# Preparation of a cross-attention and FFN kernel: one product of the query and key weights, x in two halves, the first context turned between the groups of x

## The chip, the cores and the metric

The kernel runs on one core of a Trainium2 chip. The time is the device time of one execution in microseconds (us). The core has five engines that run their own instruction streams and meet at semaphores: TensorE (PE; its weight loads are shown as PEld), VectorE (DVE), ScalarE (ACT), GpSimd (POOL) and SyncE (SP), which here only issues the DMAs.

## What is computed

x is 32 batches of 56 tokens of 128 channels; each batch has a context of 1500 rows of 128. The first stage is attention of the normalised x over the context, with a residual:

```python
    def _L0_xattn_ref(x1, x2, x3, Wq, bq, Wk, bk, Wv, bv):
        q = jnp.einsum('bsc,dc->bsd', x1, Wq) + bq
        k = jnp.einsum('bsc,dc->bsd', x2, Wk) + bk
        v = jnp.einsum('bsc,dc->bsd', x3, Wv) + bv
        scores = jnp.einsum('bqd,bkd->bqk', q, k)
        attn = jax.nn.softmax(scores, axis=-1)
        return jnp.einsum('bqk,bkd->bqd', attn, v)
...
    x = x + _L0_xattn_ref(_layernorm(x, axis=-1), ctx_1024, ctx_1024, ...)
    x = x + _L0_ffn_ref(_layernorm(x, axis=-1), ...)
```

The second stage, a gated attention of 16 heads over the 56 tokens, is not touched by the change. The kernel never forms the keys: the scores are (Wk^T(Wq y + bq)) times the context plus a term of bk that is the same along a row. So what the context is multiplied with is "qk", 128 channels by 1792 tokens (32 batches of 56).

## The kernel before

Two batches form a pair; there are 16 pairs. Tokens of batch b of a pair lie on partitions 64b to 64b+55 of `x_all`, pair n in columns 128n to 128n+127. Four pairs are a group (NG = 4 groups). All float32 data that meets the context goes as two float16 parts, high and low, three products each.

Preparation, in the order of the engines' streams:
- GpSimd fills x_all with zeros (L339), makes the identity (L340, L342), fills qT, tmax, p16, aoT and others (L345 to L361). When all groups of x are normalised it multiplies all of them by the key bias (L401), makes the low parts of contexts 0 and 1 (`low_rows`, L366), and after all four low halves of qk copies pair 0's queries (`queries`, L382).
- SP waits for the zeros of x_all, then loads x (L285, 2 x 448 KB), six weights and biases on one semaphore d_w (L289), four contexts (L293 to L295), the weights of the second stage (L309).
- DVE casts the identity (L606, L608), copies bk and, after `d_w`, the bias products (L636); for each group of x statistics and normalisation (`ln_stats`, `ln_apply`, L616 to L631); then the value bias on x (L644), constants diag_h and diag_e (L648, L649), the low half of qk (L652), low parts of contexts 0 and 1 (`split_lo`, L658), evacuation of their transposes (`t_evac`, L664), key bias of all pairs (L748, L750).
- ACT evacuates the two transposed weights (L417, L418), takes the roots (L421), evacuates the transposed x (L424), the queries (L429) and the high half of qk (L433); then casts contexts 0 and 1 (`split_hi`, L439) and evacuates transposes (`t_evac`, L444).
- TensorE transposes Wq and Wv (L923, L924), makes the bias products (L927, L928), transposes the four groups of x (L936), multiplies by Wq (L941), by Wk (L944), waits for all four low halves, and transposes contexts 0 and 1 (`turn`, L965: three chunks of 8 transposes each).

Then `steps(0)`, a loop over i = 1..6 and `steps(7)`, two pairs in each. For a pair: `scores` of its two batches (L980 to L982), the maxima (`tile_max`, L669), their transpose (`max_turn`, L988), the maximum per row and the shifts (`shifts`, m_q L675), `shift` (L996), the exponentials on ACT (`exps`, L450, L452), their low part on GpSimd (`low_probs`, L372), the values of the pair before (L1011 to L1021), and in between the turning of the next pair's contexts (`turn`, `t_evac`, `split_hi`, `split_lo`, `low_rows`). The order in each stream is written out by hand; an engine that waits holds all that stands behind in its stream. A context buffer is loaded again when its three casts are done.

## Time and profile before

| | us |
|---|---|
| time, median of 3 runs (lowest, highest) | 519.33 (518.43, 520.61) |
| the profiled execution | 519.12 |
| its span | 517.2 |
| first score matmul, pair 0 | 43.20 |
| m_q of pair 0 / of pair 3 (L675) | 48.99 / 82.42 |
| last exponentials of the attention start (ACT L452) | 216.00 |

The page gives PE 83% of the span, DVE 85%, ACT 64%, GpSimd 28%, but these are means over stages. In 40 slices of 12.9 us:

```
PE   0456888899888998856879999999999999999975
DVE  4997688888888888557989999999999999999942
POOL 8172477667777677500000000000000000000000
```

Each digit is the busy share in tenths. The first three slices are the preparation, slice 18 the join of the stages. A row of a timeline names the engine, the line, what is written <- what is read, the count of merged instructions, and in brackets how long the engine had been idle and what released it.

### The profile page before, as it was taken

To read this page: it belongs to the slowest core of one execution; us is meant where nothing else is said; L and a number is where in the kernel's file an instruction comes from. 1 tells how busy PE (TensorE), PEld (TensorE's weight loads), DVE (VectorE), ACT (ScalarE), POOL (GpSimd) and SP (SyncE) were. 2 spreads that over 40 slices of the span, in tenths; PEclk is the share of its full clock that TensorE was granted. 3 is DMA by queue.
4 is the path that set the end of the run, shared out by engine and by line. 5 is a ranking of instruction groups with operands and counts; after the bars stand their busy time and mean duration, and the time that the engine had idled before them with its cause. 6 is when DMAs were issued, how large, how long until landed. Compare 5 with 4: busy or idle time off the path is not lost.

```text
span 517.2 us, 25678 instructions
## 1 busy us (share of the span) xinstructions
PE 428.7 (83%) x10768; PEld 365.1 (71%) x10768; DVE 437.6 (85%) x818; ACT 331.6 (64%) x896; POOL 142.9 (28%) x125
## 2 busy tenths in 40 slices
PE   0456888899888998856879999999999999999975
PEld 0225777777777777745768787877878778787864
DVE  4997688888888888557989999999999999999942
ACT  1362776566775667442877678766877668766771
POOL 8172477667777677500000000000000000000000
PEclk9996899999999999977899999999999999999997
DMA  7903345433455430000000000000000000000000
GB/s 164 299 16 111 124 146 179 168 122 122 139 172 167 131 122 3 3 1 1 3 3 6 2 4 4 4 0 4 4 4 4 0 4 4 4 0 4 7 8 10
DMA packets 18125, 29.45 MB, mean 57 GB/s; under 512 B 2988, under 2 KB 13996, under 8 KB 18092
## 3 DMA queue, kind: packets, MB, share of 16 engines
q1 hardware_dynamic: 18092, 28.97, 18.0%
q8 instruction: 25, 0.41, 0.3%
q14 instruction: 8, 0.07, 0.0%
HBM read 28.05 MB, written 0.92 MB: 56 GB/s over the span
## 4 chain that ended last, share of the span: by engine, by line
DVE 49%; PE 31%; issue 13%; ACT 3%; DVEq 1%; DMA 1%; SPq 1%; POOL 1%; ACTq 0%; POOLq 0%
DVE ctxf_all L864 8%; PE ps L965 6%; DVE ctxf_all L838 6%; DVE ah L892 3%; DVE attnf L875 3%; PE ps L996 3%; DVE ctxT L664 3%; PE ps L1171 2%; PE ps L1011 2%; PE ps L1013 2%; PE ps L1012 2%; PE ps L1021 2%; PE ps L980 1%; DVE eq L790 1%; DVE eq L805 1%
## 5 line engine op out<-in xcount | busy, mean ns | idle before, releaser
L366 POOL TENSOR_TENSOR nat<-ctxf_all,nat 128x640 f16<-128x640 f32 x32 | 69.7, 2197 | 50.2 <-ACT nat L439 50.2
L527 ACT ACTIVATE e_sb<-ps,smn 128x56 f32<-128x56 f32 x256 | 76.1, 369 | 1.2 <-DVE smn L882 1.2
L965 PE MATMUL ps<-ident,nat 128*128 128x128 f16 x768 | 61.3, 226 | 11.7 <-DVE ctxT L664 5.5
L439 ACT CAST nat<-ctxf_all 128x1536 f16<-128x1536 f32 x32 | 45.5, 1470 | 39.2 <-PE ps L1013 39.2
L527 ACT ACTIVATION_READ_ACCUMULATOR e_sb<-ps,smn 128x1 f32 x256 | 67.0, 270 | 0.0
L965 PEld LDWEIGHTS ps<-ident,nat 128*128 128x128 f16 x768 | 46.6, 101 | 24.9 <-issue 14.0
L864 DVE TENSOR_TENSOR ctxf_all<-mixp,diag_h 128x3584 f16<-128x3584 f16 x32 | 63.2, 2016 | 0.0
L372 POOL TENSOR_TENSOR p<-pf,p 128x672 f16<-128x672 f32 x32 | 46.1, 1459 | 13.0 <-ACT pf L452 13.0
L444 ACT COPY ctxT<-ps 128x1024 f16<-128x1024 f16 x32 | 33.1, 1034 | 21.8 <-PE ps L965 21.8
L664 DVE COPY ctxT<-ps 128x1024 f16<-128x1024 f16 x64 | 42.6, 684 | 5.0 <-PE ps L965 5.0
L980 PE MATMUL ps<-qk_cur,ctxT 128*128 128x56 f16 x384 | 33.8, 188 | 12.4 <-DVE ctxT L664 10.5
L1106 PE MATMUL ps<-xn,mT 128*128 128x112 f16 x256 | 41.7, 220 | 0.0
L1107 PE MATMUL ps<-xn,mT 128*128 128x112 f16 x256 | 41.6, 220 | 0.0
L1108 PE MATMUL ps<-xn,mT 128*128 128x112 f16 x256 | 41.6, 220 | 0.0
L658 DVE TENSOR_TENSOR nat<-ctxf_all,nat 128x896 f16<-128x896 f32 x32 | 41.2, 1291 | 0.1
L980 PEld LDWEIGHTS ps<-qk_cur,ctxT 128*128 128x128 f16 x384 | 30.7, 96 | 15.1 <-issue 11.7
L1134 PE MATMUL ps<-ctxf_all 128*64 128x224 f16 x768 | 40.0, 260 | 0.7 <-issue 0.6
L1134 PEld LDWEIGHTS ps<-ctxf_all 128*64 128x64 f16 x768 | 36.1, 110 | 2.5 <-issue 1.4
L669 DVE TENSOR_REDUCE tmax<-ps 128x56 f32<-128x672 f32 x32 | 27.1, 850 | 11.2 <-PE ps L982 11.0
L1011 PE MATMUL ps<-p,nat 128*128 128x56 f16 (+1 forms) x384 | 33.4, 187 | 0.9 <-POOL p L372 0.9
L981 PE MATMUL ps<-qk_cur,ctxT 128*128 128x56 f16 x384 | 33.6, 188 | 0.0
L982 PE MATMUL ps<-qk_cur,ctxT 128*128 128x56 f16 x384 | 33.5, 188 | 0.0
...
## 6 DMA issues: line engine op xcount, KB each, us to landing
...
```

The lines of the kernel that those rows point to most:

```text
L366: pool.tensor_tensor(nat[k][:, 1, 7 * C:], ctxf[k][:, 7 * C:], nat[k][:, 0, 7 * C:], ALU.subtract).then_inc(natlo2, 1)
L372: pool.tensor_tensor(p16[:, 1, :, b, 0:S], pf[b][:, :, :], p16[:, 0, :, b, 0:S], ALU.subtract).then_inc(plo, 1)
L439: act.copy(nat[k][:, 0, :], ctxf[k][:, :]).then_inc(nathi, 1)
L527: last = act.activation(e_sb[:, k, b, 0:S], ps[:, b, S * k:S * k + S], ACT.Exp, bias=smn[:, K16 * b + k:K16 * b + k + 1], scale=-1.0, accu ...
L664: dve.tensor_copy(ctxT[b][:, 8 * P * c:8 * P * (c + 1)], ps[:, (3 * b + c) % 2, :].bitcast(F16)).then_inc(tev_d, 1)
L864: last = dve.tensor_tensor(dv[:, part, :, :, :], mixp[:, part, :, :].unsqueeze(2).broadcast_to((P, 2 * NQ, HALF, H)), diag_h[:, :, :].unsq ...
L965: last = pe.transpose(ps[:, (3 * b + c) % 2, :].bitcast(F16)[:, P * (j % 8):P * (j % 8) + P], nat[k][:, j // TK, C * (j % TK):C * (j % TK) ...
L980: pe.matmul(o, hi, qh, start=(t % 6 == 0), stop=False, skip_group_check=True)
L1011: pe.matmul(o, hi, ph, start=(t == 0), stop=False)
L1106: pe.matmul(o, mT[:, 0, h, :], xn16[:, 0, :], start=True, stop=False)
L1107: pe.matmul(o, mT[:, 0, h, :], xn16[:, 1, :], start=False, stop=False)
L1134: last = pe.matmul(o, pj[:, a, k, :], dv[:, b, k, :, 8 * par:8 * par + 8], start=(k % 2 == 0 and a + b == 0), stop=(k % 2 == 1 and a == 1))
```

## The change

The query and key weights are multiplied into one 128 x 128 matrix `wqk` (and Wk^T bq into a column `qk_bias`), so that qk comes from x in one product instead of two; qT and its fill are gone. x is loaded in two halves of eight pairs each, with a semaphore each, behind the weights; DVE fills the second half with zeros, and the fill of x is no longer ahead of the weights' loads. bv has its own load and semaphore, behind context 1. The constants ident16, diag_q, diag_h and diag_e are cast on ACT. Groups 2 and 3 of x are normalised by GpSimd (`apply`). The value bias and the products with the key bias are done by group on GpSimd, those for pair 0 before `steps(0)` and the rest in pairs 0 to 3; the key bias' sum (`key_bias`) is done by group on DVE. The four groups' transposes (`x_turn`) and products (`x_qk`), their evacuations (`x_evac`, `qk_evac`) and low halves (`qk_low`) stand between the pieces of the first contexts' turning; groups 2 and 3 stand in pair 0. GpSimd and DVE have `steps(1)` written out ahead of their loops. The diff, cut (`...` marks what is left out, also within a line):

```diff
@@ semaphores, sync engine @@
-        d_x = sem("d_x")
+        d_x = [sem(f"d_x{h}") for h in range(2)]
+        d_bv = sem("d_bv")
...
+        GC = NP * C // NG
+        T_BANK, Q_BANK = (2, 3, 6, 6), (6, 7, 7, 7)
...
-            sp.wait_ge(c_zero, 1)
-            for b in range(2):
-                sp.dma_start(x_all[SLOT * b:SLOT * b + S, :].rearrange("t (p c) -> t p c", c=C), x_v[b]).then_inc(d_x, 16)
-            for dst, src in ((wq_nat[:, :], wq), (wk_nat[:, :], wk), (wv_nat[:, :], wv),
+            for dst, src in ((wq_nat[:, :], wq), (wk_nat[:, :], wk), (bq_col[:, :], bq.rearrange("(d o) -> d o", o=1)),
...
+            sp.wait_ge(x_zero, 2)
+            for h in range(2):
+                for b in range(2):
+                    sp.dma_start(x_all[SLOT * b:SLOT * b + S, 2 * GC * h:2 * GC * (h + 1)].rearrange("t (p c) -> t p c", c=C),
+                                 x_v[b][:, NP // 2 * h:NP // 2 * (h + 1), :]).then_inc(d_x[h], 16)
...
+            load(0, 0)
+            load(1, 1)
+            sp.dma_start(bv_all[:, :], bv.rearrange("(o d) -> o d", o=1).broadcast_to((P, C))).then_inc(d_bv, 16)
+            load(2, 2)
+            load(3, 3)
@@ gpsimd @@
-            pool.memset(x_all[:, :], 0.0).then_inc(c_zero, 1)
+            pool.memset(x_all[:, 0:2 * GC], 0.0).then_inc(x_zero, 1)
...
-            pool.memset(qT[:, :, :], 0.0).then_inc(c_zero, 1)
...
+                if isinstance(pair, int):
+                    pool.wait_ge(qk_lo, pair // 4 + 1)
                 pool.tensor_copy(qk_cur[s][:, :, :], qk_all[:, :, bass.ds(pair * (2 * S), 2 * S)]).then_inc(qkc, 1)
...
                     low_probs(n + 1, 1, pair)
+                    if isinstance(pair, int) and pair < 4:
+                        add_bv(pair)
+                        if pair < 3:
+                            bias_products(pair + 1)
...
-            pool.tensor_tensor(x2_all[:, :].rearrange("p (n c) -> p n c", c=C), y_all[:, :].rearrange("p (n c) -> p n c", c=C),
-                               bkq[:, 0:C].unsqueeze(1).broadcast_to((P, NP, C)), ALU.mult).then_inc(xbk, 1)
+            def apply(g):
+                pool.wait_ge(ln_rstd, g + 1)
+                for n in range(4 * g, 4 * g + 4):
+                    last = pool.tensor_scalar(y_all[:, C * n:C * n + C], x_all[:, C * n:C * n + C], mv_all[:, 2 * n:2 * n + 1],
+                                              st_rstd[:, n:n + 1], ALU.subtract, ALU.mult)
+                last.then_inc(ln_xp, 1)
+            def bias_products(g):
...
+                pool.tensor_tensor(x2_all[:, k]..., y_all[:, k]..., bkq..., ALU.mult).then_inc(xbk, 1)
+            def add_bv(g):
...
+                pool.tensor_tensor(x_all[:, k]..., x_all[:, k]..., bv_all..., ALU.add).then_inc(c_xbv, 1)
             low_rows(0, 0)
             low_rows(1, 1)
-            pool.wait_ge(su_dve, NG)
             queries(0, 0)
+            apply(2)
+            bias_products(0)
+            apply(3)
             steps(0)
-            with pool.Fori(1, NP // 2 - 1) as i:
+            steps(1)
+            with pool.Fori(2, NP // 2 - 1) as i:
@@ scalar @@
+            act.wait_ge(c_id, 2)
+            act.copy(ident16[:, :], ident[:, :]).then_inc(c_cast, 1)
...
+                act.copy(diag_h[r, :, :], cut.broadcast_to((32, HALF, H))).then_inc(c_cast, 1)
+                act.copy(diag_e[r, :, :], cut.broadcast_to((32, HALF, E // 2))).then_inc(c_cast, 1)
+            act.wait_ge(w_pe, 1)
+            act.copy(wqk[:, :], ps[:, 0, 0:C]).then_inc(w_act, 1)
+            act.copy(qk_bias[:, :], ps[:, 0, C:C + 1]).then_inc(w_act, 1)
+            act.wait_ge(w_pe, 2)
+            act.copy(wvT[:, :], ps[:, 1, 0:C]).then_inc(w_act, 1)
...
+                act.activation(qk_all[:, 0, GW * g:GW * (g + 1)], ps[:, Q_BANK[g], 0:GW], ACT.Identity,
+                               bias=qk_bias[:, 0:1]).then_inc(qk_hi, 1)
...
+            deviations(0)
+            deviations(1)
             split_hi(0, 0, 0)
+            x_evac(0)
+            deviations(2)
+            qk_evac(0)
             split_hi(1, 1, 0)
+            x_evac(1)
+            deviations(3)
             t_evac(0, 0)
+            qk_evac(1)
+            x_evac(2)
             t_evac(1, 1)
+            qk_evac(2)
+            x_evac(3)
+            qk_evac(3)
@@ vector @@
-            dve.tensor_copy(ident16[:, :], ident[:, :]).then_inc(c_dve, 1)
...
+            dve.memset(x_all[:, 2 * GC:], 0.0).then_inc(x_zero, 1)
...
+                dve.wait_ge(d_x[g // 2], 32)
...
-            dve.tensor_tensor(v3(x_all), v3(x_all), bv_all[:, :].unsqueeze(1).broadcast_to((P, NP, C)), ALU.add).then_inc(c_xbv, 1)
...
+                dve.scalar_tensor_tensor(qk_all[:, 1, GW * g:GW * (g + 1)], ps[:, Q_BANK[g], 0:GW], qk_bias[:, 0:1],
+                                         qk_all[:, 0, GW * g:GW * (g + 1)], op0=ALU.add, op1=ALU.subtract).then_inc(qk_lo, 1)
...
                     tile_max(n, pair, 0)
+                    if first:
+                        qk_low(2)
+                        t_evac(1, 1, 2)
                     tile_max(n + 1, pair, 1)
+                    if first:
+                        key_bias(0)
+                        qk_low(3)
...
+                    if isinstance(pair, int) and 0 < pair < 4:
+                        key_bias(pair)
@@ tensor @@
-            pe.transpose(ps[:, 0, 0:P], wq_nat[:, :], ident[:, :])
-            pe.transpose(ps[:, 0, P:2 * P], wv_nat[:, :], ident[:, :]).then_inc(su_pe, 1)
+            pe.matmul(ps[:, 0, 0:C], wq_nat[:, :], wk_nat[:, :], start=True, stop=True)
+            pe.matmul(ps[:, 0, C:C + 1], wk_nat[:, :], bq_col[:, :], start=True, stop=True).then_inc(w_pe, 1)
+            pe.transpose(ps[:, 1, 0:C], wv_nat[:, :], ident[:, :]).then_inc(w_pe, 1)
...
+            def x_turn(g):
+                if g < 2:
+                    pe.wait_ge(ln_x, g + 1)
+                else:
+                    pe.wait_ge(ln_xp, g - 1)
+                    pe.wait_ge(qk_lo, 1)
+                    pe.wait_ge(xt_act, g)
...
+            def x_qk(g):
+                pe.wait_ge(w_act, 1)
+                pe.wait_ge(xt_act, g + 1)
+                if g >= 2:
+                    pe.wait_ge(qk_lo, g)
+                pe.matmul(ps[:, Q_BANK[g], 0:GW], wqk[:, :], xn1T[:, GW * g:GW * (g + 1)], start=True, stop=True).then_inc(qk_pe, 1)
...
                     scores(n + 1, pair, s, 1)
+                    if first:
+                        x_turn(3)
+                        x_qk(3)
+                        pe.wait_ge(qk_lo, NG)
```

TensorE's stream at the start of the program, before (ps is PSUM, ident the identity; L936 x, L941 and L944 the two products, L965 contexts 0 and 1, L980 the first scores):

```order
L923 MATMUL ps<-ident,wq_nat 128x128
L924 MATMUL ps<-ident,wv_nat 128x128
L927 MATMUL ps<-wq_nat,bk_rep 128x128
L928 MATMUL ps<-bq_col,bk_rep 128x1
L936 MATMUL ps<-ident,y_all 128x128 x16
L941 MATMUL ps<-xn1T,wqT 128x448 x4
L944 MATMUL ps<-qT,wk_nat 128x448 x4
L965 MATMUL ps<-ident,nat 128x128 x48
L980 MATMUL ps<-qk_cur,ctxT 128x56
```

The same place in the changed kernel (L1025 x, L1034 the one product, L1052 the contexts, nat0 and nat1 being contexts 0 and 1):

```order
L1012 MATMUL ps<-wq_nat,bk_rep 128x128
L1013 MATMUL ps<-bq_col,bk_rep 128x1
L1025 MATMUL ps<-ident,y_all 128x128 x4
L1052 MATMUL ps<-ident16,nat0 128x128 x8
L1034 MATMUL ps<-xn1T,wqk 128x448
L1052 MATMUL ps<-ident16,nat0 128x128 x8
L1025 MATMUL ps<-ident,y_all 128x128 x4
L1052 MATMUL ps<-ident16,nat0 128x128 x8
L1034 MATMUL ps<-xn1T,wqk 128x448
L1052 MATMUL ps<-ident16,nat1 128x128 x8
```

The groups of x now stand one by one between the chunks of the contexts, and the first scores follow when only groups 0 and 1 and four of six chunks are done.

TensorE between the scores of pair 0's two batches in the changed kernel (L1067 to L1069 are the score matmuls; before, L980 to L982 ran on without anything between):

```order
L1069 MATMUL ps<-qk_cur,ctxT 128x56
L1025 MATMUL ps<-ident,y_all 128x128 x4
L1052 MATMUL ps<-ident,nat 128x128 x8
L1034 MATMUL ps<-xn1T,wqk 128x448
L1052 MATMUL ps<-ident,nat 128x128 x8
L1067 MATMUL ps<-qk_cur,ctxT 128x56
```

Group 2 of x and the last two chunks of context 1 stand there now; group 3 stands behind the second batch's scores.

DVE from the last normalisation to the first maxima, before:

```order
L644 TENSOR_TENSOR x_all<-x_all,bv_all 128x2048
L648 CAST diag_h<-ident 32x448
...
L652 TENSOR_TENSOR qk_all<-ps,qk_all 128x448 x4
L658 TENSOR_TENSOR nat<-ctxf_all,nat 128x896 x2
L664 COPY ctxT<-ps 128x1024 x4
L748 TENSOR_REDUCE cq_x<-x_all 128x16
L750 TENSOR_SCALAR cq<-cq_x,bkq 128x16
L669 TENSOR_REDUCE tmax<-ps 128x56 x2
L675 TENSOR_REDUCE m_q<-ps 128x1
```

DVE in the changed kernel from the statistics of group 3 to m_q (L688 to L695 statistics, L729 `t_evac`, L723 `split_lo`, L711 `qk_low`, L734 `tile_max`, L716 and L718 `key_bias`, L740 m_q):

```order
L695 TENSOR_SCALAR st_ve<-mv_all 128x4
L729 COPY ctxT<-ps 128x1024
L723 TENSOR_TENSOR nat<-ctxf_all,nat 128x896
L700 RECIPROCAL st_rstd<-st_std 128x4
L711 SCALAR_TENSOR_TENSOR qk_all<-ps,qk_bias,qk_all 128x448
L729 COPY ctxT<-ps 128x1024
L734 TENSOR_REDUCE tmax<-ps 128x56
L711 SCALAR_TENSOR_TENSOR qk_all<-ps,qk_bias,qk_all 128x448
L729 COPY ctxT<-ps 128x1024
L734 TENSOR_REDUCE tmax<-ps 128x56
L716 TENSOR_REDUCE cq_x<-x_all 128x4
L718 TENSOR_SCALAR cq<-cq_x,bkq 128x4
```

The value bias and the constants are gone from DVE, one batch's maxima stand between the low halves of groups 1 and 2, and the key bias' sum is a quarter as wide.

## Rows read from the trace of the kernel before

**Rows 1.** Busy time by stage: start:end, length, per engine busy (instructions), clock, DMA, GB/s.
```profile
0.00:43.00 43.00, 17.23 (x85) 11.53 (x86) 32.42 (x79) 14.56 (x24) 22.78 (x32) 0.93 0.63 175
...
60.00:290.00 230.00, 195.53 (x4638) 168.31 (x4635) 189.76 (x373) 147.50 (x268) 114.14 (x88) 0.96 0.26 84
```

**Rows 2.** Chain of waits, first 60 us: start, us, what.
```profile
6.98 4.93 DMA bv_all<-in_L_xattn_bv_dram
...
13.76 0.79 DVE bst_all L616 x4
...
16.66 1.11 DVE y_all L631 x4
...
24.29 2.29 DVE x_all L644
26.58 4.62 DVE diag_h L648
...
33.00 2.22 DVE qk_all L652 x4
35.22 3.70 DVE nat L658 x2
...
44.14 2.20 DVE cq_x L748
...
48.99 0.30 DVE m_q L675
```

**Rows 3.** Timeline: start, us, engine, line, what, count, idle before and releaser.
```profile
3.17 1.80 POOL L345 MEMSET qT<- 128x2048 f32 x1
3.25 5.02 DVE L606 CAST ident<-ident 128x128 f16<-128x128 f32 x1 [3.25 <-POOL ident L342]
...
24.41 6.54 POOL L401 TENSOR_TENSOR x_all<-y_all,bkq 128x2048 f32<-128x2048 f32 x1 [12.01 <-DVE y_all L631]
...
31.36 0.38 DVE L648 CAST diag_h<-ident 32x448 f16<-32x448 f32 x1
```

**Rows 4.** Timeline, the loads of x on SP's queue.
```profile
2.57 0.96 SPq L285 DMA_DIRECT2D x_all<-in_x_dram  x2
```

**Rows 5.** DMA issues: KB each, median us from issue to landing.
```profile
fws_nat<-in_L_ffn_Ws_dram SPq DMA_DIRECT2D x1, 64.0 KB, 2.8
```

**Rows 6.** Busy time by stretch, columns as in rows 1.
```profile
4.00:10.00 6.00, 0.00 (x0) 0.00 (x0) 4.49 (x3) 0.00 (x0) 5.83 (x18) 1.00 1.02 175
10.00:22.00 12.00, 3.54 (x14) 2.66 (x14) 8.49 (x50) 2.50 (x8) 2.40 (x4) 1.00 1.05 339
...
38.00:44.00 6.00, 4.32 (x49) 4.04 (x50) 3.45 (x5) 1.84 (x3) 1.14 (x1) 0.50 0.75 255
...
48.00:54.00 6.00, 5.14 (x32) 3.71 (x33) 4.06 (x8) 1.60 (x2) 0.16 (x1) 0.50 0.26 77
...
60.00:62.00 2.00, 1.98 (x72) 1.86 (x69) 1.41 (x6) 1.57 (x2) 0.03 (x1) 1.00 0.04 8
```

**Rows 7.** Timeline of TensorE's weight loads, and its transposes at 39.66 us.
```profile
26.71 0.34 PEld L941 LDWEIGHTS ps<-xn1T,wqT 128*128 128x128 f32 x1 [0.41 <-issue]
...
28.05 0.19 PEld L941 LDWEIGHTS ps<-xn1T,wqT 128*128 128x128 f32 x1 [0.18 <-issue]
...
39.66 3.75 PE L965 MATMUL ps<-ident,nat 128*128 128x128 f16 x32 [2.27 <-DVE ctxT L664]
```

**Rows 8.** Instructions on tile ctxf_all up to 45 us: duration ns min/median/max.
```profile
L366 POOL TENSOR_TENSOR nat<-ctxf_all,nat x2: 1402/1818/2234, 34.4 to 35.7; 128x640 f16<-128x640 f32 x2
```

**Rows 9.** Timeline of ACT, 40 to 56 us.
```profile
43.50 2.85 ACT L439 CAST nat<-ctxf_all 128x1536 f16<-128x1536 f32 x2
52.38 1.01 ACT L444 COPY ctxT<-ps 128x1024 f16<-128x1024 f16 x1 [6.04 <-PE ps L965]
```

**Rows 10.** Timeline of DVE and of GpSimd in pairs 2 and 3.
```profile
70.31 0.86 DVE L669 TENSOR_REDUCE tmax<-ps 128x56 f32<-128x672 f32 x1 [0.71 <-PE ps L982]
...
72.80 2.32 POOL L366 TENSOR_TENSOR nat<-ctxf_all,nat 128x640 f16<-128x640 f32 x1 [2.92 <-ACT nat L439]
```

More of the change, by code:

```diff
@@ L699, in result @@
                 after(dve, x2c, pair)
+                if isinstance(pair, int) and pair < 4:
+                    dve.wait_ge(c_xbv, pair // 4 + 1)
                 after(dve, prj, pair + 1)
@@ L902, in iteration @@
                     second(i + 1)
-            dve.wait_ge(c_zero, 22)
+            dve.wait_ge(c_zero, 21)
+            dve.wait_ge(c_cast, 11)
             dve.wait_ge(x2c, NP)
@@ L1057, in steps @@
                         turn(n + 3, 1, k1, (2,))
-            for b in range(2):
-                turn(b, b, b)
+            x_turn(0)
+            pe.wait_ge(c_cast, 1)
+            pe.wait_ge(w_act, 3)
+            pe.wait_ge(bkq_out, 1)
+            turn(0, 0, 0, (0,))
+            x_qk(0)
+            turn(0, 0, 0, (1,))
+            x_turn(1)
+            turn(0, 0, 0, (2,))
+            x_qk(1)
+            turn(1, 1, 1, (0,))
+            pe.wait_ge(c_zero, 9)
             steps(0)
```

180 lines of the change are left out of this document (93 added, 87 removed).

## The prediction

> **What bounds the kernel now.** I read the busy shares by stage first, then the chain of waits, then the timelines of the engines on it. The kernel has a preparation of 43 us, sixteen pairs of attention up to about 215 us, and a second stage. In the preparation no engine is full: DVE is busy 32 of 43 us, PE 17, ACT 15 [rows 1]. From 60 us on DVE and PE hold each other above 80%, and the change leaves the code of that stretch alone but for four pairs. So the time to win is the time before the first pair.
>
> The chain [rows 2] says why the preparation is long: it goes through DVE nearly all the way. After the landing of the last weight (11.9 us) DVE normalises x, then does on the path, among other things, the value bias on all of x (2.29), the casts of the constants (4.62 for the first alone), the low half of the queries for all pairs (2.22), both low halves of the contexts (3.70), and the key bias of all pairs (2.20); for three of these five pair 0 needs only a quarter of it, or nothing yet. The reduction of pair 0's maxima, m_q, starts at 48.99. I take it as the end of the preparation and ask when it starts afterwards.
>
> The 4.62 and a 5.02 us cast at 3.25 us are stalls, not work: the same cast takes 0.38 when GpSimd is idle, and both long ones lie under GpSimd's own instructions, a row of fills and a 6.54 us multiply [rows 3].
>
> **The loads.** Before, SP waits for the fill of x_all and issues x at 2.57 us, the weights after it, 0.48 us each [rows 4]. Now five weight loads go first and wait for nothing. I start them at 0.75 us, where the first fill starts today: issued by 3.1. A small weight load takes 2.8 us from issue to landing [rows 5], so the last one is there at about 5.4 instead of 11.9. Packets of x move at 175 GB/s, those of the contexts at 339 and more [rows 6]. x in two halves of 0.46 MB behind the weights, stream starting at 4.2, 2.6 us each, 0.8 us for the landing (an estimate: from the last packets to the release at 11.9): halves at 7.6 and 10.2, context 0 (0.77 MB, 2.1 us at an estimated 370, since the 339 holds smaller packets too) at 12.2, context 1 at 14.3. The bias load bv now stands behind context 1; its reader is GpSimd in pair 0, much later.
> Fresh here is the fill of x's second half on DVE. No row shows a DVE fill. Lower bound: half of GpSimd's 1.80 for 2048 columns [rows 3], 0.9 us, done before SP gets there at 3.1, so free. Upper bound: it is held like the cast, until GpSimd's row of fills pauses (8.27 us before; 5.6 now, since 1.8 us of qT and 0.9 us of x are gone), which makes x 2.5 us later. I take free, as a fill reads nothing; the held case is a rival. The Trainium skill, "VectorE: DVE Perf Modes", section "Zero memsets can be issued as uint32 (trn2)", has such a fill at one cycle per element, by which it would be an estimated 1.1 us; no run here shows it.
>
> **Weights and x.** The two transposes become one product of the weights, the product with bq and one transpose; two evacuations become three small ones. They fall in 5.4 to 7.6 us where all wait for x: nothing. Then DVE's first two statistics and first normalisation, 4.1 us (13.7 to 17.8 [rows 2]): y of group 0 at 11.7, 6.1 us earlier than now. ACT's casts of constants (about 4 us) run from 2.4 us on, and w_pe is waited for only after: hidden by the loads; without that cover they would cost those 4 us.
>
> **The interleaved part.** Here each engine waits for the next, in order, so I followed the instruction order of the new kernel with today's durations. At the low clock, as PE has it at 26 us (weight loads of the 448-column product 0.74 apart, 0.37 at the high clock, each the load and the idle time ahead of it; two loads per product [rows 7]), x_qk takes 1.5, at the high clock 0.75. Eight context transposes take 0.94 (32 in 3.75 [rows 7], at 0.50 of the clock) or an estimated 0.6, 36 score matmuls 1.0 at the high clock (72 in 1.98 [rows 6]) or an estimated 1.7.
> ACT casts context 0 at 12.2 to 13.7 (two take 2.85 [rows 9]). Then x_qk(0) ends 16.3, its evacuation and low half 17.8 (0.6 each, as the four low halves in 2.22 [rows 2], and a release of 0.1 to 0.2 ahead of each). DVE normalises group 1 till 16.7, so x_turn(1) ends 18.6. DVE's statistics of group 3 end at 19.9, and ACT's deviations(3) waits for them with t_evac(0,0) behind it: till 21.1. x_qk(1) ends 21.0, its low half 22.5, t_evac(1,1,0) 23.2. scores(0) can start at about 22.
> Between scores(0) and scores(1) now stands new work: x_turn(2), a context turn, x_qk(2), their evacuations, low half and t_evac, and behind scores(1) the same for group 3, with max_turn waiting for all four low halves. At the low clock throughout: scores(1) 29.7 to 31.4, x_turn(3) to 32.7, x_qk(3) to 34.9, low half 36.3, m_q at 36.9. With the clock up from 21 us (PE is busy nearly without gap from 14 on): scores(1) ends 28.8, low half 32.7, m_q 33.3. I take 35.0 between them, as there are gaps of over 1 us while DVE and ACT work. **Gain: 48.99 - 35.0 = 14.0 us**, bounds 12.1 and 15.7.
>
> **What is late next.** The casts of contexts 2 and 3 stood at 43.5 us [rows 9], well ahead of m_q. Now they stand behind qk_evac(3), so the low half of context 2 meets GpSimd's part of it. In such a meeting the GpSimd part took up to 2.23 us, the lone one 1.40 [rows 8], and DVE's two 3.70 [rows 2]: 0.2 to 1.4 us, I take 0.8. t_evac of context 2 on ACT was already 3.4 us behind m_q [rows 9], so the rest keeps its distance.
> Here the Trainium skill speaks against the change ("SBUF — State Buffer", section "SBUF: two separate sides"): GpSimd and a DVE instruction with two SBUF inputs or in its fast mode take one port pair in turn, the later blocked for the whole instruction. The trace agrees: one context pair serialised. By that rule nothing in my sum is free where the added GpSimd pieces meet split_lo, and the sum would be nearer its upper bounds.
>
> **In pairs 0 to 3.** key_bias(1..3) puts a reduction of 512 columns and a small add, some 0.9 us by the 2.20 for 2048, ahead of tile_max. The second tile_max waits 0.71 us for PE [rows 10], which covers most: 0.2 each, 0.6 together; bounds 0 and 2.7. The seven quarter pieces on GpSimd (add_bv, bias_products): 512 columns cost 1.12 by the lone 1.40 for 640, 1.64 by the 6.54 for 2048. Two per pair are 2.2 to 3.3, and GpSimd waits 2.92 per pair [rows 10]: 0 to 0.4 for each of three, I take 0.5 in all. apply(2) and apply(3) end well ahead of x_turn(2) and (3).
> PE ran at 1.2 GHz through 48 to 54 us [rows 6]; if it comes in warm this saves up to 2 us of transposes and shifts; I take 0.5.
>
> **Sum.** 519.1 us of the profiled execution (span 517.2; the median is 519.3, so the same): -14.0 + 0.8 + 0.6 + 0.5 - 0.5 = -12.6, **506.5 us**.
>
> **Rivals.**
> The fill is held: x at 10.1, everything behind it 2.5 later: 509.0. For: the 5.02 us cast. Against: it reads nothing. Chance 0.12.
> The interlock binds: clock low to the end and every meeting at its dearer bound: -12.1 + 1.4 + 1.4 + 1.1 + 0: 510.9. For: the clock at 38 to 44 us was 0.50 [rows 6]; many hops, each of which can lose 0.1 us of release. Chance 0.22.
> The clock rises early and stays: -15.7 + 0.2 + 0.3 + 0 - 1.5: 502.4. For: PE denser than today. Against: the waits for groups 2 and 3. Chance 0.13.
> It doesn't do what it says: the first pairs wait for something else (contexts 2 and 3, the ones in order behind them) and the gain is given back, within 0.5%: 519. Against: all four contexts landed by 19 us by the rates above. Chance 0.03.
> Slower: GpSimd becomes the bound in pairs 0 to 3. Its pieces delay low_rows of the next contexts, and PE's third turn waits for these. Today it has 2.9 us to spare; to eat the 14 us over four pairs its two pieces would need 2.9 + 3.5 = 6.4 us, 3.2 each; for 0.5% slower, 3.9 each: 522. The dearest row gives 1.64. Chance 0.02.
> The forecast keeps 0.48.
>
> **Numbers.** Range 502 to 511.5: it reaches from the early clock to the interlock, and allows for the join of the two stages (214 to 256 us), where a shift by 13 us meets the clock's changes elsewhere. 0.5% is 2.6 us, about what a measurement can tell: faster 0.95, same 0.03, slower 0.02.
>
> **What would show it.** x's first statistics on DVE at about 7.6 us (10.1: held fill). No long cast on DVE. First scores at 21 to 23 us. scores(1) 6 to 8 us behind scores(0). m_q at 33 to 37. The same distance of m_q from pair to pair as before from pair 4 on, and pairs 1 to 3 within 0.5 of it; if they take more, look whether GpSimd's wait ahead of low_rows is gone. The forecast is wrong if the context casts on ACT start well behind 12.2 us, or if PE waits for qk_lo longer than 4 us ahead of max_turn.

## The result

The changed kernel takes 510.15 us (median of 4 runs, 509.59 to 512.48) beside 519.97 for the kernel before in the same comparison: ratio 0.983, 95% interval 0.981 to 0.986. Its profiled execution took 509.82 us, with a span of 508.0. So 9.3 us are gone between the two profiled executions, where 12.6 were predicted; 510 lies inside the range of 502 to 511.5, at its slow end.

The stages, against [rows 1] (start:end, length, per engine busy (instructions), clock, DMA, GB/s):

```profile
0.00:43.00 43.00, 22.69 (x194) 16.74 (x194) 27.34 (x74) 21.91 (x37) 23.92 (x42) 0.88 0.67 195
60.00:290.00 230.00, 194.45 (x4735) 166.76 (x4733) 194.12 (x373) 148.37 (x296) 110.85 (x87) 0.97 0.23 77
```

DVE does 5 us less and ACT 7 us more in the first 43 us, and TensorE is turning pair 1's contexts by then. The chain of waits of the changed kernel (start, us, what), where [rows 2] had DVE:

```profile
4.55 0.46 SPq L299
5.05 0.88 SPq L304
5.97 0.32 SPq L305
6.34 6.55 DMA ctxf_all<-in_ctx_dram
12.91 1.48 ACT nat L501
...
15.54 1.61 PE ps L1034 x2
17.24 0.64 ACT qk_all L494
17.91 0.68 DVE qk_all L711
...
24.71 0.99 PE ps L1025 x4
...
34.58 0.30 DVE m_q L740
34.90 1.40 DVE nshift L742
36.33 1.37 DVE dg L746
```

Up to 12.9 us it is now the loading of context 0; of x only the issuing of its loads is on it (L299), not its landing. Then it passes between ACT, PE and DVE, and m_q of pair 0 stands at 34.58: 14.4 us ahead of before, where 14.0 was predicted. The rest of the story is behind m_q. Its two followers, nshift and dg, which take 0.22 and 0.25 us in a quiet pair, took 1.39 and 1.36.

Start of m_q (us) in the two kernels, and its distance to the next:

| pair | before | after | lead | distance before | distance after |
|---|---|---|---|---|---|
| 0 | 48.99 | 34.58 | 14.41 | 11.73 | 14.04 |
| 1 | 60.72 | 48.62 | 12.10 | 10.87 | 11.58 |
| 2 | 71.59 | 60.20 | 11.39 | 10.83 | 10.83 |
| 3 | 82.42 | 71.03 | 11.39 | 10.83 | 11.89 |
| 4 | 93.25 | 82.92 | 10.33 | 10.84 | 11.61 |
| 5 | 104.09 | 94.53 | 9.56 | 10.86 | 10.83 |
| 15 | 212.06 | 202.45 | 9.61 | | |

So 4.8 us are given back in pairs 0 to 4, 2.3 in pair 0 and 2.5 in the next four, and nothing later; from the last m_q to the end of the span it is 305.1 us before and 305.5 after.

### The profile page after: what moved, and what is told of

It is laid out like the page before. It is cut to its first block, busy times and chain, and to the rows that moved or that the text cites. A ratio compares the mean times of both kernels' runs of the same rounds, so it can differ in the third digit from the quotient of the medians.

```text
span 508.0 us, 25659 instructions
## 1 busy us (share of the span) xinstructions
PE 424.5 (84%) x10763; PEld 362.0 (71%) x10763; DVE 428.5 (84%) x805; ACT 333.6 (66%) x904; POOL 149.6 (29%) x139
## 4 chain that ended last, share of the span: by engine, by line
DVE 48%; PE 30%; issue 14%; ACT 4%; DVEq 1%; DMA 1%; SPq 1%; POOL 0%; ACTq 0%; POOLq 0%
DVE ctxf_all L947 8%; DVE ctxf_all L921 6%; PE ps L1052 6%; DVE ah L975 3%; DVE attnf L958 3%; DVE ctxT L729 3%; PE ps L1083 3%; PE ps L1279 2%; PE ps L1098 2%; PE ps L1099 2%; PE ps L1100 2%; PE ps L1108 1%; DVE oh L894 1%; DVE eq L873 1%; DVE eq L888 1%
## 5 line engine op out<-in xcount | busy, mean ns | idle before, releaser
L379 POOL TENSOR_TENSOR nat<-ctxf_all,nat 128x640 f16<-128x640 f32 x32 | 67.0, 2110 | 45.4 <-ACT nat L501 45.2
L1052 PE MATMUL ps<-ident,nat 128*128 128x128 f16 x768 | 61.0, 225 | 11.7 <-DVE ctxT L729 3.4
L1052 PEld LDWEIGHTS ps<-ident,nat 128*128 128x128 f16 x768 | 46.4, 100 | 27.1 <-issue 16.1
L1067 PE MATMUL ps<-qk_cur,ctxT 128*128 128x56 f16 x384 | 34.3, 189 | 12.8 <-DVE ctxT L729 10.8
L729 DVE COPY ctxT<-ps 128x1024 f16<-128x1024 f16 x64 | 42.8, 685 | 2.4 <-PE ps L1052 2.4
L723 DVE TENSOR_TENSOR nat<-ctxf_all,nat 128x896 f16<-128x896 f32 x32 | 42.1, 1315 | 1.3 <-ACT nat L501 1.2
L1067 PEld LDWEIGHTS ps<-qk_cur,ctxT 128*128 128x128 f16 x384 | 30.9, 96 | 15.6 <-issue 10.5
L1214 PE MATMUL ps<-xn,mT 128*128 128x112 f16 x256 | 40.3, 217 | 0.0
L1215 PE MATMUL ps<-xn,mT 128*128 128x112 f16 x256 | 40.1, 216 | 0.0
L1216 PE MATMUL ps<-xn,mT 128*128 128x112 f16 x256 | 40.1, 216 | 0.0
L734 DVE TENSOR_REDUCE tmax<-ps 128x56 f32<-128x672 f32 x32 | 27.0, 851 | 11.0 <-PE ps L1069 11.0
L1068 PE MATMUL ps<-qk_cur,ctxT 128*128 128x56 f16 x384 | 34.0, 188 | 0.0
L1069 PE MATMUL ps<-qk_cur,ctxT 128*128 128x56 f16 x384 | 34.0, 188 | 0.0
```

The lines of the kernel that those rows point to most:

```text
L379: pool.tensor_tensor(nat[k][:, 1, 7 * C:], ctxf[k][:, 7 * C:], nat[k][:, 0, 7 * C:], ALU.subtract).then_inc(natlo2, 1)
L723: dve.tensor_tensor(nat[k][:, 1, 0:7 * C], ctxf[k][:, 0:7 * C], nat[k][:, 0, 0:7 * C], ALU.subtract).then_inc(natlo, 1)
L729: dve.tensor_copy(ctxT[b][:, 8 * P * c:8 * P * (c + 1)], ps[:, (3 * b + c) % 2, :].bitcast(F16)).then_inc(tev_d, 1)
L1052: last = pe.transpose(ps[:, (3 * b + c) % 2, :].bitcast(F16)[:, P * (j % 8):P * (j % 8) + P], nat[k][:, j // TK, C * (j % TK):C * (j % TK) ...
L1067: pe.matmul(o, hi, qh, start=(t % 6 == 0), stop=False, skip_group_check=True)
L1214: pe.matmul(o, mT[:, 0, h, :], xn16[:, 0, :], start=True, stop=False)
```

## Where the 4.8 us go: two engines at one time

The timelines of DVE and of GpSimd behind m_q of pair 0 in the changed kernel (start, us, engine, line, what, count, idle before and releaser):

```profile
34.58 0.29 DVE L740 TENSOR_REDUCE m_q<-ps 128x1 f32<-128x128 f32 x1 [0.42 <-PE ps L1075]
34.90 1.39 DVE L742 SCALAR_TENSOR_TENSOR nshift<-m_q,cq 128x1 f32<-128x1 f32 x1
36.33 1.36 DVE L746 TENSOR_SCALAR dg<-diag_q,nshift 128x56 bf16<-128x56 f32 x1
37.73 0.30 DVE L748 SCALAR_TENSOR_TENSOR dg<-diag_q,nshift,dg 128x56 bf16<-128x56 f32 x1
...
34.88 2.76 POOL L379 TENSOR_TENSOR nat<-ctxf_all,nat 128x640 f16<-128x640 f32 x2 [5.91 <-ACT nat L501]
```

GpSimd had sat idle for 5.91 us, waiting for ACT's casts of contexts 2 and 3, and began its two low parts (1.38 each) 0.02 us ahead of nshift. nshift ends when the first of them ends, dg when the second does. Each works on one or 56 columns; the 2.3 us are the wait for GpSimd.

In pair 3 it is the order of two starts that decides. First pair 3 of the changed kernel, then pair 4, then pair 5, from when on the distances are the old ones:

```profile
71.36 0.39 DVE L742 SCALAR_TENSOR_TENSOR nshift<-m_q,cq 128x1 f32<-128x1 f32 x1
...
72.26 2.29 DVE L723 TENSOR_TENSOR nat<-ctxf_all,nat 128x896 f16<-128x896 f32 x1
...
72.18 3.64 POOL L379 TENSOR_TENSOR nat<-ctxf_all,nat 128x640 f16<-128x640 f32 x2 [0.45 <-ACT nat L501]
...
83.90 1.48 DVE L748 SCALAR_TENSOR_TENSOR dg<-diag_q,nshift,dg 128x56 bf16<-128x56 f32 x1
...
83.91 3.74 POOL L379 TENSOR_TENSOR nat<-ctxf_all,nat 128x640 f16<-128x640 f32 x2 [1.68 <-ACT nat L501]
...
106.52 1.09 DVE L723 TENSOR_TENSOR nat<-ctxf_all,nat 128x896 f16<-128x896 f32 x1
...
106.56 4.52 POOL L379 TENSOR_TENSOR nat<-ctxf_all,nat 128x640 f16<-128x640 f32 x2 [2.92 <-ACT nat L501]
```

In pair 5 DVE comes 0.04 us ahead, takes 1.09, and GpSimd waits at no cost (the same in the kernel before: DVE's low half at 72.77 with 1.08, and GpSimd at 72.80 [rows 10]). In pair 3 GpSimd comes 0.08 us ahead and DVE's low half takes 2.29. Pair 1 is the same (GpSimd 0.04 us ahead, the low half 2.30), and pair 2, with the same added work, escapes by 0.05 us. In pair 4 the two meet one instruction earlier: the second part of dg takes 1.48 where it takes 0.28 in pair 5. Its start is 0.01 us ahead of GpSimd's in the profile, which is too little to say who was first. The shift is small: ACT's cast, which releases GpSimd, began 0.35 us ahead of m_q in such a pair before, and 0.41 ahead in pair 3 now. DVE in turn is late by `key_bias` or by a GpSimd piece (nshift took 0.39). GpSimd's idle time ahead of these low parts, 2.92 us in both kernels' quiet pairs, is 0.45 in pair 3.

By the Trainium skill ("SBUF — State Buffer", section "SBUF: two separate sides") an instruction of GpSimd and one of DVE that wants the shared port pair lock each other out for a whole instruction, and whoever starts first has it. The trace agrees: 1.39 us for nshift beside a GpSimd instruction of 1.38 that had begun 0.02 us earlier, and 1.09 or 2.29 for the same low half by who came first. Pair 4, above, neither bears this out nor speaks against it.

My theory from here, **A**: the missing 3 us are these meetings, so they come back when GpSimd's low parts, or its pieces, stand elsewhere. The rival, **B**: pairs 0 to 4 are late by something else on their way (the late casts and turnings of contexts 2 and 3, or the added `key_bias` sums on DVE), and a held instruction only fills a wait.

## Experiments on the first pairs

Each kernel is the changed one with the edit shown, unless it says otherwise. The changed kernel itself was run a second time, in one comparison with "contexts 2 and 3 cast earlier", "GpSimd told to wait" and "the pieces of pairs 0 to 3": 508.71 us, ratio 0.982 (0.979 to 0.985), m_q of pair 0 at 34.33 and the distances as above within 0.01 us. The experiments of this section differ from it by about 2 us, and only for the pieces is the interval of the ratio apart from its own. So the readings below rest on the distances between the m_q, from one profile for each kernel, and not on the times.

**Contexts 2 and 3 cast earlier.** ACT casts them between the evacuations of qk (and no longer in pair 0; that part of the edit isn't shown), so that GpSimd's low parts fall ahead of m_q.

```diff
             qk_evac(1)
+            split_hi(2, 2, 0)
             x_evac(2)
             t_evac(1, 1)
             qk_evac(2)
+            split_hi(3, 3, 0)
             x_evac(3)
```

> ACT casts contexts 2 and 3 in its idle times of pair 0 (behind qk_evac(1) and qk_evac(2)), not behind qk_evac(3). Theory A, the port: in pair 0 DVE's two small instructions nshift (1.39 us, else 0.22) and dg (1.36, else 0.25) are held by GpSimd's low parts of contexts 2 and 3, which start 0.3 us behind m_q; with the casts early GpSimd is done before m_q, both take their usual time, m_q of pair 1 comes 2.3 us earlier (46.3), and the time falls by 2.0 to 2.5 us (ratio 0.979). Rival B, the clock and the table: pair 0 is long because TensorE runs at half clock and ACT loads a table; then m_q of pair 1 moves by less than 0.5 us.

Measured: 506.93 us, ratio 0.976 (0.972 to 0.981); m_q 34.26, 45.89, 57.47. Behind m_q of pair 0:

```profile
34.59 0.22 DVE L745 SCALAR_TENSOR_TENSOR nshift<-m_q,cq 128x1 f32<-128x1 f32 x1
34.84 0.25 DVE L749 TENSOR_SCALAR dg<-diag_q,nshift 128x56 bf16<-128x56 f32 x1
...
28.99 2.77 POOL L379 TENSOR_TENSOR nat<-ctxf_all,nat 128x640 f16<-128x640 f32 x2
```

Pair 0's distance fell from 14.04 to 11.63 (11.73 before the change), the others stayed at 11.58, 10.82, 11.88, 11.62. All 2.4 us of pair 0 go with the meeting. The time fell by 1.8 us, where 2.0 to 2.5 were expected.

**GpSimd told to wait.** That kernel also moves the casts. Here the casts stay, and GpSimd alone starts its low parts in pair 0 later, behind dg.

```diff
+                        if first:
+                            pool.wait_ge(dgr, 1)
                         low_rows(n + 2, (2 * s + 2) % 4)
```

> In pair 0 GpSimd waits for the end of DVE's shifts before the low part of context 2. Theory A, the port: nshift and dg take 0.22 and 0.25 us, the low part of GpSimd comes 1 us later and now meets DVE's low part, so 1.0 to 2.3 us are won in pair 0 and m_q of pair 1 comes at 46.3 to 47.6. Rival B: the two are slow for another reason (their operands, the first use): they stay at 1.4 us each, and the time stays or rises.

Measured: 506.84 us, ratio 0.978 (0.974 to 0.981); pair 0's distance 11.57.

```profile
34.31 0.22 DVE L744 SCALAR_TENSOR_TENSOR nshift<-m_q,cq 128x1 f32<-128x1 f32 x1
34.56 0.25 DVE L748 TENSOR_SCALAR dg<-diag_q,nshift 128x56 bf16<-128x56 f32 x1
34.85 0.28 DVE L750 SCALAR_TENSOR_TENSOR dg<-diag_q,nshift,dg 128x56 bf16<-128x56 f32 x1
35.04 1.08 DVE L725 TENSOR_TENSOR nat<-ctxf_all,nat 128x896 f16<-128x896 f32 x1
...
35.21 4.38 POOL L379 TENSOR_TENSOR nat<-ctxf_all,nat 128x640 f16<-128x640 f32 x2 [6.47 <-DVE dg L750]
```

Nothing was moved ahead, an engine was made to wait, and pair 0 lost 2.5 us all the same (1.0 to 2.3 were expected). GpSimd's two low parts now take 4.38 instead of 2.76, at no cost in pair 0. This separates A from B for pair 0: it was neither the late casts nor the turning. But pair 2 of this kernel took 11.74 us instead of 10.83: there GpSimd came 0.08 us ahead of DVE's low half, which took 2.29, the meeting that pair 2 of the changed kernel had escaped. From pair 0 to pair 5 the gain is 1.5 us, and not 2.5.

**The pieces of pairs 0 to 3.** GpSimd does the key bias products of groups 1 to 3 and the value bias of group 0 ahead of `steps(0)`, and the other value biases one pair earlier.

```diff
             apply(3)
+            bias_products(1)
+            bias_products(2)
+            bias_products(3)
+            add_bv(0)
             steps(0)
...
-                    if isinstance(pair, int) and pair < 4:
-                        add_bv(pair)
-                        if pair < 3:
-                            bias_products(pair + 1)
+                    if isinstance(pair, int) and pair < 3:
+                        add_bv(pair + 1)
```

> The four products with the key bias and the first value-bias piece are done by GpSimd in its idle 6 us before pair 0's low parts; pairs 0 to 2 keep one value-bias piece each, the key-bias sums on DVE stay. From m_q of pair 1 to that of pair 5 the changed kernel takes 45.9 us where the kernel before takes 43.4. Theory A, GpSimd's pieces: they hold a small DVE instruction or push DVE's low part behind GpSimd's; without most of them at least half of the 2.5 us is gone, and the time falls by 1.3 to 2.5. Rival B, the key-bias sums on DVE (0.9 us in each of three pairs): they stay, so the 45.9 stays within 0.4.

Measured: 506.69 us, ratio 0.977 (0.974 to 0.979); from m_q of pair 1 to that of pair 5 44.35 us, where it was 45.91 after the change and 43.37 before. So 1.6 of the 2.5 us went with these pieces. Pair 4 still took 11.61. But a piece that is moved meets DVE where it lands, here ahead of m_q:

```profile
31.86 2.19 DVE L720 TENSOR_SCALAR cq<-cq_x,bkq 128x4 f32<-128x4 f32 x1
33.96 0.67 DVE L713 SCALAR_TENSOR_TENSOR qk_all<-ps,qk_bias,qk_all 128x448 f16<-128x448 f32 x1
...
29.06 3.73 POOL L432 TENSOR_TENSOR x_all<-y_all,bkq 128x512 f32<-128x512 f32 x3
32.74 1.28 POOL L443 TENSOR_TENSOR x_all<-x_all,bv_all 128x512 f32<-128x512 f32 x1
```

A 4-column instruction (0.23 in the changed kernel) was held for the rest of one GpSimd piece and the whole of the next, and m_q of pair 0 was at 35.05.

**Casts, pieces and sums all in pair 0.** The early casts; GpSimd's products 1 to 3 and value biases 0 and 1 behind the shifts of pair 0, and DVE's `key_bias` 1 to 3 in the gaps of pair 0, so that pairs 1 to 3 have nothing of the sums left. Pairs 1 and 2 keep one value bias piece each.

```diff
+                    if first:
+                        pool.wait_ge(dgr, 1)
+                        for g in range(1, 4):
+                            bias_products(g)
+                        for g in range(2):
+                            add_bv(g)
                     low_probs(n, 0, pair)
...
-                    if isinstance(pair, int) and 0 < pair < 4:
-                        key_bias(pair)
```

> Early casts of contexts 2 and 3 as before, and all pieces of pairs 1 to 3 moved into pair 0, behind DVE's shifts: the key-bias products and two value-bias pieces on GpSimd, the key-bias sums in DVE's waits. Two value-bias pieces stay, in pairs 1 and 2. Theory A, GpSimd's pieces and DVE's sums together move GpSimd's low parts ahead of DVE's in pairs 1 to 4: m_q of pair 1 at 46 to 46.5 us, from pair 1 to pair 5 43.4 us as in the kernel before (45.9 in the changed one), the time 4 to 5 us below the changed kernel's: 504, ratio 0.972. Rival B, the unrolled second pair of steps or the loads of the contexts cost it: 45.9 stays.

Measured: 506.8 us, ratio 0.978 (0.974 to 0.983); m_q 34.23, 46.66, 57.88, 68.71, 79.53, 90.36. From pair 1 to 5 it is 43.70 us, within 0.33 of the kernel before (43.4 expected), and rival B, by which 45.9 would stay, is out: the pieces and the sums together were 2.2 of the 2.5 us. In these pairs this kernel has the same pieces as the one before it but not the sums, so about 0.65 of it (44.35 to 43.70) were the sums; the early casts alone had left it at 45.90. Pair 0 took 12.43 instead of 11.63. At the last m_q this kernel is 1.3 us ahead of the early casts alone (198.32 and 199.59), and the time doesn't show it. My expectation of the time, 504 us and 4 to 5 below the changed kernel, missed: it was about 2 below, and a gain of 1 us at the last m_q is not resolved by 4 runs. From the last m_q to the end of the span, the profiled executions of all these kernels took between 304.4 and 307.3 us, with code that is the same.

## Experiments on the preparation

**The kernel before with the constants cast on ACT.** The one part of the change that the stalls of [rows 3] speak for, done alone in the kernel before.

```diff
-            dve.tensor_copy(ident16[:, :], ident[:, :]).then_inc(c_dve, 1)
+            act.wait_ge(c_id, 2)
+            act.copy(ident16[:, :], ident[:, :]).then_inc(c_dve, 1)
```

(and diag_q, diag_h, diag_e in the same way)

> The kernel before with one part of the change: the constants are cast on ACT. Theory A, a chain beside a chain: ACT's high halves of qk end at 32.9 us and its cast of context 0 at 34.3 in any case, and DVE has only 0.9 us on them; the stalls of 5.02 and 4.62 us go, but m_q of pair 0 comes only 0.3 to 1.2 us earlier (48.0) and the time falls by as much. Rival B, the stalls are on the path as the chain of waits has them: 6 us earlier (43), the time with it.

Measured: 518.23 us beside 518.78, ratio 0.999 (0.998 to 1.001); m_q of pair 0 at 48.19 instead of 48.99. Both stalls, 5.02 and 4.62 us, are gone, and DVE waits in their place:

```profile
24.29 2.29 DVE L649 TENSOR_TENSOR x_all<-x_all,bv_all 128x2048 f32<-128x2048 f32 x1
31.42 2.88 DVE L652 TENSOR_TENSOR qk_all<-ps,qk_all 128x448 f16<-128x448 f32 x4 [4.83 <-ACT qk_all L442]
```

The two longest stalls of the profile were worth 0.8 us at m_q, and the time doesn't show that much. The way x, q, qk through TensorE and ACT was nearly as late as DVE, so the 14.4 us of the change can't come from the casts alone. Its first statistics on DVE start 6.0 us earlier (13.67 before, 7.70 after), and the other 8.4 are won behind them. How they divide between the product that is gone and the new order of the groups and contexts is not shown: no run takes one of these alone.

**x awaited whole.** The statistics of the first two groups wait for both halves.

```diff
-                dve.wait_ge(d_x[g // 2], 32)
+                dve.wait_ge(d_x[0], 32)
+                dve.wait_ge(d_x[1], 32)
```

> The changed kernel, but the statistics of group 0 wait for both halves of x. If the second half lands 2.5 us behind the first, they start at about 10.2 us and not at 7.7. Theory A, the path goes over context 0: its landing (12.9 us) and cast (14.4) hide most of it, and m_q of pair 0 comes 1.0 us later (bounds 0.5 and 1.5). Rival B, the path goes over x: m_q 2.5 us later.

Measured: 512.76 us, ratio 0.989 (0.985 to 0.992). With the halves the ratio was 0.983 and 0.982 in two sets; the intervals just touch, so the 0.6% between them is barely resolved. The statistics start at 10.51 instead of 7.70, but the first maxima at 24.91 instead of 24.84: context 0's landing covers nearly all of it, as A said. Yet m_q of pair 0 came at 36.82, 2.2 us later than with halves, where A gave 1.0 (at most 1.5). A's number missed, and B's 2.5 is nearer, though not by B's way. Two rows show where:

```profile
25.89 1.11 PE L1026 MATMUL ps<-ident,y_all 128*128 128x128 f32 x4 [1.12 <-POOL y_all L422]
26.79 1.06 PE L1053 MATMUL ps<-ident,nat 128*128 128x128 f16 x8
27.67 1.79 PE L1035 MATMUL ps<-xn1T,wqk 128*128 128x448 f32 x2
```

TensorE waited 1.12 us for GpSimd's `apply(2)`, and the granted clock was 0.50 at 26 to 28 us, 1.2 GHz, and x_qk(2) took 1.79 where it took 0.99 after the change.

**Group 2 ahead of context 1's last chunk, with and without GpSimd's part.** ACT evacuates context 0's second chunk ahead of `deviations(3)`; the scores of batch 0 hang on it.

```diff
             x_evac(1)
-            deviations(3)
             t_evac(0, 0)
+            deviations(3)
```

> ACT evacuates the first context transpose before the roots of group 3, for which it idles 1.1 us. Theory A, GpSimd's normalisation of group 2 (3.61 us, done at 24.6 us in the changed kernel) is next: scores of pair 0 start 1 us earlier, the transposes of group 2 hardly earlier, m_q of pair 0 gains 0 to 0.3 us. Rival B, the ACT wait alone is on the path: m_q 1.0 us earlier (33.5).

Measured in one run: 510.95 us, and m_q of pair 0 at 36.87, 2.3 us later than after the change. Both theories missed. The first maxima did come earlier (23.71 instead of 24.84), but in the changed kernel `apply(2)` ended at 24.62 and x_turn(2) started at 24.68, with no slack; now TensorE waited 2.05 us for it. Then the clock fell (granted 0.66 at 26 to 28 us and 0.50 from 28 to 42). So a next kernel adds one move on GpSimd: `apply(2)` directly behind the low rows of context 0, ahead of those of context 1.

```diff
             low_rows(0, 0)
-            low_rows(1, 1)
-            queries(0, 0)
             apply(2)
+            queries(0, 0)
+            low_rows(1, 1)
```

> As the swap of t_evac(0,0) and deviations(3), and besides GpSimd does apply(2) directly behind the low rows of context 0, ahead of the queries and of the low rows of context 1. In the swap alone GpSimd is free from 16.9 to 19.4 us and apply(2) (3.61) starts only at 21.15, and TensorE waits 2.05 us for it at 24.81. Theory C (the 2.3 us that the swap lost came by this one wait and by the lower granted clock that followed it): apply(2) runs from 17.9 to 21.5, the wait ahead of x_turn(2) is under 0.4, the granted clock stays 1.00 until about 35, x_qk(3) takes 0.99, m_q at 33.2 to 33.8. Theory D (the clock falls there for another reason, and the wait only went along with it): clock 0.50 from 27 on again, x_qk(3) 1.8, m_q at 35.5 or later.

Measured in one run: 507.64 us, m_q of pair 0 at 32.30. TensorE at the third group, first with the swap alone, then with `apply(2)` moved too (the third group's transposes there start at 22.7, without a wait):

```profile
24.81 0.66 PE L1025 MATMUL ps<-ident,y_all 128*128 128x128 f32 x4 [2.05 <-POOL y_all L422]
...
26.14 1.33 PE L1034 MATMUL ps<-xn1T,wqk 128*128 128x448 f32 x2 [0.22 <-issue]
...
33.02 1.83 PE L1034 MATMUL ps<-xn1T,wqk 128*128 128x448 f32 x2 [0.67 <-issue]
```

```profile
23.98 0.99 PE L1034 MATMUL ps<-xn1T,wqk 128*128 128x448 f32 x2 [0.22 <-issue]
...
29.44 0.99 PE L1034 MATMUL ps<-xn1T,wqk 128*128 128x448 f32 x2 [0.67 <-issue]
```

x_qk(2) comes 2.2 us earlier, which is the wait, and m_q 4.6 us earlier; the other 2.4 go with TensorE at 2.4 instead of 1.2 GHz (granted clock 1.00 up to 34 us). It even beat the range of 33.2 to 33.8 by 0.9. GpSimd's `apply(2)` took 3.14 us in the new place and 3.61 in the old.

**Both together, and all.** The early casts with this order of ACT and GpSimd; and the same with the pieces and sums in pair 0.

> The casts of contexts 2 and 3 early on ACT, together with the swap and the early apply(2). Theory C: m_q 33.2 to 33.8, and the pairs as with the early casts alone (11.6, 11.6, 10.8, 11.9, 11.6), so the last m_q 0.8 to 1.0 ahead of 199.6: 505.9 us, ratio 0.974 to 0.977. Theory D: m_q at 35.5 or later, 508.3, ratio 0.979 to 0.982.

> The same, and the pieces and key bias sums of pairs 1 to 3 in pair 0, behind the shifts. Theory C: m_q 33.2 to 33.8, pair 0 12.4 as in that variant, the others 43.7 up to pair 5, the last m_q at about 197.5: 504.5 us if the second stage takes what it takes after the changed kernel (305.5), ratio 0.971 to 0.976. Rival: the m_q of the last pair comes forward by that and the time does not follow (it did not follow by more than 0.1 us when the last m_q went from 199.6 to 198.3): 506.5 to 507.

Measured: 505.32 us, ratio 0.975 (0.973 to 0.978), and 503.68 us, ratio 0.972 (0.970 to 0.974). Both ratios lie in the ranges expected, and the rival, that the time would not follow the last m_q (506.5 to 507 us), is out for the second kernel, the last of all. That one is 14.7 us, or 2.8%, below the kernel before in its own comparison (518.33) and beats the changed kernel by about 1.1%: the intervals 0.970 to 0.974 and 0.981 to 0.986 are apart. m_q of pair 0 was at 32.17 and 33.33 (33.2 to 33.8 expected). Their streams are the same up to there, and one row tells them apart, x_qk(3) in the first and in the second:

```profile
29.16 0.99 PE L1037 MATMUL ps<-xn1T,wqk 128*128 128x448 f32 x2 [0.67 <-issue]
```

```profile
29.48 1.83 PE L1045 MATMUL ps<-xn1T,wqk 128*128 128x448 f32 x2 [0.67 <-issue]
```

and the stretches of 28 to 32 us, again in the first and in the second (columns as in [rows 1]; the clock is the third number from the end):

```profile
28.00:30.00 2.00, 1.33 (x6) 0.55 (x5) 1.97 (x3) 0.53 (x1) 2.00 (x2) 1.00 0.83 290
30.00:32.00 2.00, 0.49 (x3) 0.28 (x3) 1.52 (x2) 0.63 (x1) 0.81 (x2) 0.75 0.16 59
```

```profile
28.00:30.00 2.00, 1.33 (x11) 0.95 (x8) 1.78 (x3) 0.53 (x1) 2.00 (x3) 0.72 0.82 303
30.00:32.00 2.00, 1.31 (x2) 0.00 (x0) 1.15 (x1) 0.59 (x1) 1.13 (x2) 0.50 0.15 52
```

The clock fell to 1.2 GHz inside 30 to 32 us in the first and inside 28 to 30 in the second, with the same work and from 20 us on the same waits ahead of it, 0.3 us apart. So its fall in the swapped kernel can't be laid to the 2.05 us wait alone. What is shown is the wait itself (2.05 us in one row) and the price of a fall (0.8 us here, x_qk(3) at 1.83 instead of 0.99, the rest of the 1.2 us at m_q being the 0.3 that was there before it; up to 2.4 in the swapped kernel). Whether the wait brought the fall is open; a profile of each of several executions would be needed.

All runs together (m_q in us, from the profiled execution). The times come from four comparisons, in which the kernel before took 519.97, 518.64, 518.78 and 518.33 us; each ratio is to its own comparison's, so compare ratios and not times:

| kernel | m_q pair 0 | pair 5 | pair 15 | time | ratio to before |
|---|---|---|---|---|---|
| before | 48.99 | 104.09 | 212.06 | 519.97 | 1 |
| after | 34.58 | 94.53 | 202.45 | 510.15 | 0.983 |
| after, second set | 34.33 | 94.26 | 202.10 | 508.71 | 0.982 |
| early casts | 34.26 | 91.79 | 199.59 | 506.93 | 0.976 |
| GpSimd told to wait | 33.98 | 92.38 | 200.12 | 506.84 | 0.978 |
| pieces early | 35.05 | 92.72 | 200.47 | 506.69 | 0.977 |
| all in pair 0 | 34.23 | 90.36 | 198.32 | 506.80 | 0.978 |
| before, casts on ACT | 48.19 | 103.29 | 211.26 | 518.23 | 0.999 |
| x awaited whole | 36.82 | 96.61 | 204.43 | 512.76 | 0.989 |
| swap | 36.87 | 96.65 | 204.52 | 510.95 | one run |
| swap and `apply(2)` | 32.30 | 92.23 | 200.06 | 507.64 | one run |
| that, early casts | 32.17 | 89.86 | 197.64 | 505.32 | 0.975 |
| that, all in pair 0 | 33.33 | 89.47 | 197.25 | 503.68 | 0.972 |

## The prediction, point by point

The sum against the two profiled executions: 14.4 us gained up to m_q of pair 0 (predicted 14.0), 2.3 given back in pair 0 (0.8, and 0.5 to be gained there by the clock), 2.5 in pairs 1 to 4 (0.6 and 0.5), and 0.4 behind the last m_q, of which the sum had nothing and which is less than the spread of that stretch (304.4 to 307.3). That makes 9.2 instead of 12.6. The total came inside the range because the largest term was right; the terms behind it were too small by 3.4 us together.

**The fill and the loads: right.** DVE's fill and its first statistics:

```profile
1.03 0.91 DVE L679 MEMSET x_all<- 128x1024 f32 x1 [1.03 <-PEq L1372]
...
7.70 0.87 DVE L688 BATCH_NORM_STATS2 bst_all<-x_all 128x6 f32<-128x128 f32 x4 [0.72 <-DMA x_all<-in_x_dram]
```

The fill took 0.91 us (0.9 taken) beside GpSimd's own fill and was not held; the statistics came at 7.7 (7.6). The rival of the held fill is out. y of group 0 came at 11.8 (11.7).

**The way to m_q: right in the end, late in the middle.** Context 0's cast began at 12.91, not 12.2:

```profile
12.91 1.47 ACT L501 CAST nat<-ctxf_all 128x1536 f16<-128x1536 f32 x1 [2.09 <-DMA ctxf_all<-in_ctx_dram]
```

The second half of x, ahead of it in the queue, was there at 10.51 in the kernel that awaits it (10.2 taken), and the load itself took the rest of the 0.7 us. The first scores came at 22.8 (22), the second batch's 6.6 us later (6 to 8), m_q at 34.6 (35.0). The products and turns were dearer than taken (x_qk 1.80 and 0.99 us at the two paces, for 1.5 and 0.75), so it is partly luck that m_q came out within 0.4 us. The clock was between the two cases, as assumed, but the other way round in time: 0.52 at 22 to 24 us and 1.00 at 26 to 34. The second set had 1.00 at 22 to 24 as well, and m_q 0.25 us earlier. The granted clock alone doesn't tell the pace everywhere: it reads 1.00 from 14 to 18 us, where x_qk(0) took 1.80 and not 0.99.

**"apply(2) and apply(3) end well ahead": wrong for apply(2).** I gave no duration for them. `apply(2)` took 0.90 us per pair, 3.6 in all, and ended 0.06 us ahead of the transposes that read it. In the second set, where the scores ahead of them ran at the high clock, TensorE waited 1.12 us for it: the clock's gain on the scores was mostly lost in that wait, and m_q came only 0.25 us earlier. So a wait that I had put at nothing bounds this stretch. The swap lost 2.3 us at m_q where it had won 1.1 at the first maxima.

**"0.2 to 1.4 us, I take 0.8" for contexts 2 and 3: the step that failed.** The mechanism was named, with the rule of the two engines, and put to the wrong instructions. I priced the meeting of GpSimd's low parts with DVE's low half, as in the trace before. But they met nshift and dg, which stand ahead of it and on the path of every later pair, and each lost a whole GpSimd instruction: 2.3 us. I had followed the start of GpSimd's work (released by ACT's cast, at 34.9) only as far as "behind qk_evac(3)". My own working had m_q at 35.0 and the low half of group 3 done 0.6 us ahead of it; with 0.6 us for that low half, an estimate from it puts the end of qk_evac(3), and so the start of the casts, 1.2 us ahead of m_q, and the end of the first cast (half of 2.85) 0.2 behind it, just where nshift starts. The two kernels that moved GpSimd's start, one forward and one back, brought back 2.4 and 2.5 us of pair 0.

**"I take 0.5" for a warm TensorE in pair 0: nothing came of it.** The granted clock was 0.50 from 36 to 42 us, where the transposes and shifts stand.

**0.6 and 0.5 for pairs 0 to 3: the second term of the wrong size**, 2.5 measured, just about the dearer bounds of the second rival (1.4 and 1.1). That rival takes 1.4 for the sums, where the text gives 2.7 as their upper bound; with 2.7 it would be at 512.2 us, outside the range. The pieces took 1.27 us each, inside the 1.12 to 1.64. What failed is the thought that work inside an engine's idle time is free. It is for GpSimd; but it changes who comes first at the next meeting, by less than 0.1 us, and the one who comes second pays 1.2. The pieces were 1.6 of it, the sums about 0.65, and 0.33 stayed with both away.

**The rivals.** The interlock at its dearer bounds, 510.9 us with a chance of 0.22, is nearest to the 509.8 measured, though by another sum: m_q was 2.3 us better than it had, pair 0 0.9 worse, and 0.4 was lost behind the last m_q. The early clock (502.4) didn't come in this kernel; m_q at 33.3, which it needed, was reached only with the changed order on ACT and GpSimd. The first pairs waiting for something else (519, chance 0.03) named the right place, but 4.8 of the 14.4 us went there, not all. Slower by GpSimd: its pieces cost 1.27, not the 3.9 needed (3.6 by that paragraph's own working).
